# Ends of two attention stages and the expert gates behind them: an earlier start of the gate, banks of its own, last sums on GpSimd

## The reference

```
x = x + cross_attention(layernorm(x), context, mask)      # 16 heads of 16, masked
x = x + ffn(layernorm(x))     # self attention, then a hard choice of one of 8 experts
x = x + cross_attention(layernorm(x), context)            # no mask
x = x + ffn(layernorm(x))     # a hard choice by 256 gate columns, expert = column % 8

# layer 0's ffn, with h = layernorm(x, ln1)
u = h_in + attention(h) @ wo + bo                 # h_in is the ffn's input
hn2 = layernorm(u, ln2)
idx = argmax(hn2 @ gate_w + gate_b)               # 8 columns
out = u + relu(hn2 @ w1[idx] + b1[idx]) @ w2[idx] + b2[idx]

# layer 1's ffn, with h = layernorm(x)
probs = softmax(h @ Wg + bg); idx = argmax(probs)  # 256 columns
out = relu(h @ We[idx % 8] + be[idx % 8]) * probs[idx]
```

## Time and profile before

| | |
|---|---|
| median of 3 runs | 1204.88 us |
| lowest, highest | 1201.55, 1215.09 us |
| profiled execution | 1195.19 us |
| its span, first to last instruction | 1193.5 us |
| mean granted TensorE clock | 0.942 |
| PE busy | 1066.2 us (89%) |
| DVE busy | 758.1 us (64%) |
| ACT busy | 612.6 us (51%) |
| POOL busy | 222.2 us (19%) |

### The profile page before, as it was taken

How to read it: one execution, slowest core, us unless ns; L and a number is a source line. 1 busy time by engine, 2 the same in 40 slices (tenths; PEclk the granted TensorE clock), 3 DMA queues, 4 the chain that set the end, 5 groups by cost and what they waited for, 6 DMA issues and landing times. The chain is left out here.

```text
span 1193.5 us, 17937 instructions
## 1 busy us (share of the span) xinstructions
PE 1066.2 (89%) x5834; PEld 540.2 (45%) x5834; DVE 758.1 (64%) x1850; ACT 612.6 (51%) x1305; POOL 222.2 (19%) x360
## 2 busy tenths in 40 slices
PE   7989999999898999999859999996989999998380
PEld 4533333333454334444636666664633444436260
DVE  4777777876578898886542222124688988856632
ACT  2236666666432777777412333321337877783250
POOL 2000000000210314324222222202001112021255
PEclk9979999999998999999969999998979999999695
DMA  8954433330079454532750401003964333302064
GB/s 291 324 148 113 122 77 74 87 72 2 1 243 286 92 132 108 134 108 64 269 189 26 169 27 34 25 17 134 301 225 105 91 75 82 69 15 71 25 175 145
DMA packets 72922, 141.74 MB, mean 119 GB/s; under 512 B 9148, under 2 KB 26176, under 8 KB 71424
## 3 DMA queue, kind: packets, MB, share of 16 engines
q1 hardware_dynamic: 68752, 130.36, 37.1%
q0 software_dynamic: 4080, 10.23, 3.1%
HBM read 86.30 MB, written 52.17 MB: 116 GB/s over the span
## 5 line engine op out<-in xcount | busy, mean ns | idle before, releaser
L960 ACT ACTIVATE r<-ps 128x512 f32<-128x512 f32 x768 | 417.9, 599 | 185.0 <-PE ps L1074 184.2
L411 DVE TENSOR_REDUCE m<-ps 128x1 f32<-128x512 f32 x512 | 320.8, 683 | 47.0 <-PE ps L1043 47.0
L1074 PE MATMUL ps<-stacks 50*128 50x512 f32 x768 | 284.9, 461 | 7.9 <-DMA stacks<-mT 4.6
L1043 PE MATMUL ps<-stacks 48*128 48x512 f32 x720 | 286.4, 475 | 3.7 <-DVE r L488 3.0
L1083 PE MATMUL ps<-r 128*32 128x512 f32 x1536 | 208.0, 614 | 1.5 <-ACT r L960 1.5
L1074 PEld LDWEIGHTS ps<-stacks 50*128 50x128 f32 x768 | 121.1, 189 | 181.9 <-ACT r L960 126.6
L407 DVE CUSTOM_DVE_ANT_0 r<-ps,r 128x512 bf16<-128x512 f32 x256 | 165.9, 688 | 52.2 <-PE ps L1043 51.6
L1043 PEld LDWEIGHTS ps<-stacks 48*128 48x128 f32 x720 | 116.7, 192 | 24.1 <-DVE m L411 14.3
L886 POOL CAST mparts<-m 128x16 fp32r<-128x16 f32 x48 | 9.9, 206 | 550.1 <-DVE m L411 316.5
L614 ACT ACTIVATE r<-ps,cols 128x512 fp32r<-128x512 f32 x48 | 33.0, 688 | 115.6 <-PE ps L675 100.8
L675 PE MATMUL ps<-r,w 128*128 128x512 f32 x192 | 90.5, 609 | 0.5 <-issue 0.5
(11 more groups left out here) (152 smaller groups left out, 1115.8 us busy)
## 6 DMA issues: line engine op xcount, KB each, us to landing
stacks<-q_parts SPq DMA_DIRECT2D x96, 192.0 KB, 3.6
stacks<-k_parts SPq DMA_DIRECT2D x96, 192.0 KB, 4.4
k_parts<-r SPq DMA_DIRECT2D x24, 512.0 KB, 3.4
q_parts<-r SPq DMA_DIRECT2D x24, 512.0 KB, 4.4
r<-in_w SPq DMA_DIRECT2D x16, 512.0 KB, 3.6
r<-in_w SPq DMA_DIRECT2D x8, 1024.0 KB, 14.4
k_parts<-r SPq DMA_DIRECT2D x24, 256.0 KB, 4.0
q_parts<-r SPq DMA_DIRECT2D x24, 256.0 KB, 4.1
```

Of the source, the lines that this page charges most:

```text
L411: ins = dve.tensor_reduce(out, mem.ps[:, bank, :], AX.X, ALU.max)
L960: act.activation(mem.probs[:, u // HG, u % HG, :], ps[:, ST + unit_of(b, g, u) % DEEP, :], ACT.Exp, scale=SCALE).then_inc(a.p_exp.sem, 1)
L1043: pe.matmul(ps[:, led_bank(n), :], stack_of(mem.qst[g], h, ROWS)[:, t * P:(t + 1) * P], stack_of(mem.kst[g], h, ROWS), start=True, stop=Tr ...
L1074: pe.matmul(ps[:, ST + N % DEEP, :], stack_of(mem.kst[g], h, KROWS)[:, kt * P:(kt + 1) * P], stack_of(mem.qst[g], h, KROWS), start=not a.m ...
```

## The change

- Statistics of batches 0 and 1 move to places (2, 6) and (2, 9) of the last batch, those of batch 2 to (3, 9); the rows of batches 0 and 1 to (3, 2) and (3, 7). The rows of batch 2 stay between the last `normalise` and the residual. For this the rows move to the start of their region, onto query stacks, and wait until those are read.
- GpSimd's scale steps go into the attention's own order of GpSimd.
- The last batch's sum into `total_x` goes from DVE to GpSimd, and the copy into `x` is gone in `sa0`: the gate reads batch 3 from `block_in`.
- PE transposes batch 0 ahead of the last `turn`, and batch 1 ahead of the last output projection. Behind the stage PE's order is logits 0, logits 1, turn 2, logits 2, turn 3, logits 3.
- ACT's order is copies 0 in the stage, then copies 1, copies 2, exponentials 0, copies 3, exponentials 1, 2, 3.
- Each batch has a pair of banks for transposes and then logits: (0, 1), (5, 6), (2, 7), and (0, 1) again for batch 3.

```diff
-        self.rnT = [take(self.r3, C * S, [C, S]), self.w[0][:, 2:4, :, :].rearrange("p i c d -> p i (c d)")]
         self.rn = take(self.r3, NT * D, [B, T, D])
+        row_from = at[0]
+        self.rnT = take(self.r3, C * S, [C, S])
+        self.rnT_beside = [self.w[0][:, 2:4, :, :].rearrange("p i c d -> p i (c d)"),
+                           self.w[1][:, 0:2, :, :].rearrange("p i c d -> p i (c d)")]
...
+    def last_total(k):
+
+        two = slice(2 * k, 2 * k + 2)
+        pool.wait_ge(a.op_used.sem, a.op_used.at(B - 1, k + 1))
+        pool.wait_ge(a.acc_stored.sem, a.acc_stored.at(B - 1))
+        pool.tensor_tensor(mem.total_x[:, two, :], mem.x[:, B - 1, two, :], mem.block_in[(B - 1) % 2][:, two, :],
+                           ALU.add).then_inc(a.acc_ready.sem, 1)
...
+            if scale is not None and b == B - 1 and g == 3:
+                scale(0)
+                scale(1)
             if a.rows is not None and b and g >= 2:
                 sums(b - 1, g - 2)
+    if scale is None:
+        return
+    scale(2)
+    if a.self_block:
+        last_total(0)
+    scale(3)
+    if a.self_block:
+        last_total(1)
...
     products(G, NG - 1, T - 1)
+    if beside is not None:
+        meanwhile()
     turn(G)
-    meanwhile()
+    if beside is None:
+        meanwhile()
     for c in range(1, C):
         turn_out(B - 1, c, LAST_TURN[c])
+    if beside is not None:
+        beside()
     for t in range(T):
         project_out(B - 1, t, LAST_OUT[t // 2])
...
         dve.tensor_tensor(u, got, u, ALU.add).then_inc(a.op_used.sem, 1)
-        dve.wait_ge(a.op_used.sem, a.op_used.at(b, k + 1))
-        dve.wait_ge(a.acc_stored.sem, a.acc_stored.at(b))
-        dve.tensor_tensor(mem.total_x[:, two, :], x, u, ALU.add).then_inc(a.acc_ready.sem, 1)
-        dve.wait_ge(a.acc_ready.sem, a.acc_ready.at(b, k + 1))
-        dve.tensor_copy(x, u).then_inc(a.x_done.sem, 1)
...
+TURN_BANKS = ((0, 1), (5, 6), (2, 7), (0, 1))
...
     def normalise(b):
         dve.wait_ge(m.scale.sem, m.scale.at(b, 2))
+        dve.wait_ge(a.st_ps.sem, a.st_ps.at(NG * (B - 1) + b + 1))
...
+    steps = {
+        (2, 6): lambda: statistics(0),
+        (2, 9): lambda: statistics(1),
+        (3, 2): lambda: normalise(0),
+        (3, 7): lambda: normalise(1),
+        (3, 9): lambda: statistics(2),
+    }
 
     def between():
-        for b in range(1, early):
-            normalise(b)
+        normalise(2)
 
     def rest_of_batches():
-        for b in range(early, B):
-            statistics(b)
-        body(0)
-        for b in range(early, B):
-            normalise(b)
+        statistics(B - 1)
+        choose(0)
+        normalise(B - 1)
         for b in range(1, B):
-            body(b)
+            choose(b)
...
     def turned(b):
+        if b == 1 and a.self_block:
+            act.wait_ge(a.x_done.sem, a.x_done.at(B - 1))
+        if b >= 2:
+            act.wait_ge(m.g_ps.sem, m.g_ps.at(b - 1))
...
+    def rest_of_batches():
+        turned(1)
+        turned(2)
         if m.hidden is None:
             act.sem_inc(m.exps.sem, m.exps.lead)
-        turned(0)
-
-    def rest_of_batches():
-        for b in range(B):
-            body(b)
+            exps(0)
+        turned(3)
+        if m.hidden is None:
+            for b in range(1, B):
+                exps(b)
...
     def turn(b):
-        pe.wait_ge(m.rnT_ready.sem, m.rnT_ready.at(b))
+        if b == 1:
+            pe.wait_ge(a.oT_sb.sem, a.oT_sb.at(B - 1, 1))
+            pe.wait_ge(a.ot_sb.sem, a.ot_sb.at(B * NG))
+        if b == 2:
+            pe.wait_ge(a.oT_sb.sem, a.oT_sb.at(B))
+            pe.wait_ge(a.quotient.sem, a.quotient.at(B * NG))
+        if b == 3:
+            pe.wait_ge(m.logit.sem, m.logit.at(0, 2))
         pe.wait_ge(m.rn_ready.sem, m.rn_ready.at(b, 1))
...
     def begin():
-        pe.sem_inc(m.rnT_ps.sem, m.rnT_ps.lead)
         turn(0)
 
+    def beside():
+        turn(1)
+
     def rest_of_batches():
-
-        for b in range(B):
-            body(b)
-
-    return begin, rest_of_batches
+        logits(0)
+        logits(1)
+        turn(2)
+        logits(2)
+        turn(3)
+        logits(3)
```

More of the change, by code:

```diff
@@ L1202, in attend_tensor, with attend_vector @@
     pe.wait_ge(last.sem, last.at(B))
-def attend_vector(dve, a, meanwhile, beside=None):
+def attend_vector(dve, a, steps, beside=None):
     mem = a.mem
@@ L1259, in body @@
                     residual(b - 1, k)
-                if last and (g, u) in NEXT_STAGE:
-                    meanwhile[NEXT_STAGE.index((g, u))]()
+                if last and (g, u) in steps:
+                    steps[(g, u)]()
     for v in range(LEAD - UNITS):
@@ L1291, in __init__ @@
     def __init__(self, nc, stage, mem, dram, name, affine, gate_width, row, hidden, b2, weights,
-                 x_done, acc_stored, gathered, earlier, scattered=None, fetched=None, out_stored=None):
+                 before, rnT, gathered, earlier, scattered=None, fetched=None, out_stored=None):
         self.mem, self.dram, self.name, self.affine = mem, dram, name, affine
         self.width, self.row, self.hidden, self.b2 = gate_width, row, hidden, b2
-        self.weights, self.x_done, self.acc_stored = weights, x_done, acc_stored
+        self.weights, self.before, self.acc_stored = weights, before, before.acc_stored if hidden is not None else None
+        self.rnT = [mem.rnT, rnT]
         self.used = []
@@ L1344, in __init__, with tokens_after @@
             self.out_stored = Signal(out_stored, 16)
+TURN_BANKS = ((0, 1), (5, 6), (2, 7), (0, 1))
+def tokens_after(m, b):
+    a = m.before
+    return m.mem.block_in[b % 2] if a.self_block and b == B - 1 else m.mem.x[:, b, :, :]
 def gate_vector(dve, m):
@@ L1388, in body, with scale @@
         dve.tensor_copy(mem.expert[:, b, :], mem.expert_u[:, :]).then_inc(m.choice.sem, 1)
[L1390 to L1396, removed]
-            statistics(b)
-    def begin():
-        normalise(0)
+    steps = {
[5 more added lines that the diff above has]
+    }
     def between():
-        for b in range(1, early):
-            normalise(b)
+        normalise(2)
     def rest_of_batches():
-        for b in range(early, B):
-            statistics(b)
-        body(0)
-        for b in range(early, B):
-            normalise(b)
+        statistics(B - 1)
+        choose(0)
+        normalise(B - 1)
         for b in range(1, B):
-            body(b)
-    return start, begin, between, rest_of_batches
+            choose(b)
+    return steps, between, rest_of_batches
 def gate_gpsimd(pool, m):
     mem = m.mem
-    for b in range(B):
+    def scale(b):
         pool.wait_ge(m.aggr.sem, m.aggr.at(b, T))
@@ L1496, in begin @@
     def begin():
[L1497 removed]
         turn(0)
+    def beside():
+        turn(1)
     def rest_of_batches():
[L1502 to L1505 removed]
+        logits(0)
[4 more added lines that the diff above has]
+        logits(3)
+    return begin, beside, rest_of_batches
 COUNTS, TOKENS = 6, 7
@@ L2073, in _ @@
                 rest()
-                start, begin, between, rest = gate_vector(dve, me1)
-                attend_vector(dve, xa1, (lambda: start(xa1), lambda: (last_stack(xa1), begin())), between)
+                steps, between, rest = gate_vector(dve, me1)
+                attend_vector(dve, xa1, steps, between)
                 rest()
```

93 lines of the change are left out of this document (42 added, 51 removed).

## The result

The changed kernel takes 1208.34 us (median of 22 runs, 1205.68 to 1215.65), the kernel before 1202.83 (22 runs). The ratio is 1.0042, interval 1.0026 to 1.0059: 5.1 us slower, 3.1 to 7.1. I had forecast 3.9 us more, at 1208.8.

What follows compares the result with a forecast made beforehand. PE was taken to bound layer 0's gate, DVE and ACT layer 1's. Terms +1.8 and +2.1 us gave +3.9, added to the median 1204.88 for 1208.8 us; range 1199 to 1218.

Steps and rivals of the forecast that it cites:

- The sum: Whole kernel: +1.8 us in layer 0 and +2.1 in layer 1, +3.9 in all, giving 1208.8 us.
- The prediction's own signs: Both gates: later projection, earlier logits 0, PE and DVE gaps, exponentials behind copies; 37.6 us to gather, 37.4 to one-hot.
- Part 4, layer 1: Cross attention's gate: exponentials queue behind ACT's copies and delay DVE's choosing, +2.1 us, bounds 0.0 and +8.5.
- Part 4, layer 0: Self attention's gate: PE waits twice for its transposes' copies, logits 3 end later, +1.8 us, bounds -1.7 and +3.2.
- Part 2: Gate transposes moved in front: projections 0.5 and 0.3 us later, logits 0.45 earlier in layer 0, 0.6 in layer 1.
- Part 3: Last sums on GpSimd: batch 3's statistics about 1 us earlier, SP's stores issued up to 3.7 later, cost 0.
- rival 3: Layer 0: GpSimd's late addition delays SP, rows land after 614 and bound the gather, up to +3.7 us; chance 0.03.
- Parts 1 and 5: Early statistics and rows under the last attention groups, and own PSUM banks per batch in the gate: 0 each.
- The first: Level holds in layer 0, layer 1's logits start earlier without ACT queueing: -2.3 us, 1202.6; chance 0.22.
- The second: Layer 1: half clock level reaches past the last transposes, +6.4 us more, total 10.3, 1215.2; chance 0.13.
- The fourth: Change does less than said, early steps blocked; ends stay within 1 us of before, 1204.9; chance 0.07.
- The rule on transposes: Skill's rule that transposes do not bring PE's full rate; the prediction held layer 1's trace, level back by 1085, against it.

Runs made afterwards that it cites:

- pair of repeats: Kernel before and changed kernel, each run again unchanged for a second profile: ratios to the kernel before 1.0009 and 1.0026.
- the repeat of before: The kernel before, run once more unchanged for a second profile: ratio 1.0009 (0.9983 to 1.0035).
- e4: Changed kernel with ACT's increment for DVE early and ACT's old order, PE's new order kept: ratio to the kernel before 1.0015.
- e3: Changed kernel with ACT's increment for DVE early and gate transposes one batch ahead of the logits again: ratio to the kernel before 1.0012.
- e1: Changed kernel with only ACT's increment, which lets DVE begin choosing batch 0, back at the gate's start: ratio to the kernel before 1.0039.
- f1: e3 with both of GpSimd's last additions in layer 0 made ahead of batch 3's scale: ratio to the kernel before 0.9973.
- f3: f1 with four extra bf16 matmuls, results unused, at four places of layer 0's gate: ratio to the kernel before 0.9974.

## Why the prediction was right, point by point

**The sum** was right in sign and size: +3.9 us forecast, +5.1 measured (3.1 to 7.1). Its parts were not, and part of the hit is luck. In the pair of repeats layer 0 changes by -0.2 (forecast +1.8) and layer 1 by +4.25 (+2.1), so one term too high and one too low add up to 4.1 beside 3.9. That 1208.8 and 1208.34 nearly meet is luck as well: the forecast stood on 1204.88, a median of three runs, and the median of 22 is 1202.83.

**The prediction's own signs.** Two came: logits 0 right behind the residual, and the gaps in front of logits 2 and 3 in layer 0. The others did not. The output projection of layer 0 was not 0.5 later. From the last products to the first gather it took 39.4 and 38.9 us, not 37.6, and the repeat of before took 39.0. In layer 1 the exponentials of batch 0 did not follow the copies, the gap of about 2 us in front of batch 1's addition is absent, and the one-hot came 38.1 us behind the last products, not 37.4. By the words of the prediction absent gaps, and a level that differs over more than 3 us (it fell 10 to 11 us behind the copy, not 15.7), mean that its mechanism is wrong. For layer 1 it is.

**Part 4, layer 1**, +2.1 forecast; B rose by 3.5 on the mean of two profiles each, 2.8 on the first pair, 4.25 on the repeats. ACT's order was named as the cause, and it is (e4: 4.97 us with everything else kept). But the wait was another one. I had put the cost at exponentials 0 behind copies 2, and in the changed kernel those cost nothing. What costs is DVE's permission to begin, which stood in the same queue ahead of them: 6.41 us of idle DVE, 4.97 in B against e3. The exponentials behind copies, 2.07, show only once the increment is early (e1). The line stood in the diff. I had read it as bookkeeping, and followed only instructions that take time.

**Part 4, layer 0**, +1.8 forecast, bounds -1.7 and +3.2; +1.7 on the means, +3.6 by the first pair, -0.2 by the repeats. The two waits for copies came as forecast, 0.87 us each (0.7 to 1.3). The rest is where the level falls, 10 to 13 us behind the copy in the kernels without extra matmuls, 15.7 in the profile that I worked from. I called that fall steady ("the work before 590 hardly changes"); it is not, in the unchanged kernel either. So the forecast for layer 0 is not confirmed: the profiles give anything from -0.2 to +3.6, as the level fell in the kernel before.

**Part 2**, the head start, was sized too low: logits 0 were to start 0.45 and 0.6 earlier, and start 1.21 earlier in layer 0 (8.13 against 9.34) and 0.84 in layer 1 against the repeat, 2.27 against the first profile with its half level. The projection did not come later, as I had it, but 3.57 us behind the copy instead of 3.77: the transposes fill PE's waits for ACT and DVE, and I had added up the drawn lengths of pipelined groups.

**Part 3**, the sums on GpSimd: 0 forecast, and 0 in the changed kernel. The cover was PE's own lateness. With that gone (e3) the second addition cost 0.9 us in X through the cast that it blocked, and rival 3, the stores, set the gather (e3, f1, f3). **Parts 1 and 5** cost nothing that shows; no run here takes either out by itself.

**The rivals.** The first (level holds, nothing queues on ACT) failed: DVE waited 6.41 us for ACT's queue. The second failed: in layer 1 the last transposes and the projection ran at the full level in the changed kernel, 3.70 us for the projection. The third did not come in the changed kernel, whose gather followed the routing; it came once the routing was earlier (e3, f1, f3). The fourth failed: the time is 3.1 to 7.1 us longer, not the same within 1.

**The rule on transposes.** The prediction set it against the earlier trace rows. No run here decided it further, as the level fell at that place in no other profile.

## What to carry to other kernels

When a step is moved behind other work on its engine, follow the semaphore increments that stand in it as well: a "buffer is free" signal has no duration in the profile and can hold another engine for 6 us. Between two profiles of one kernel the length of layer 0's gate moved by 3 us with the clock's level, so take two profiles of each kernel before working out such a stretch from one, and compare those in which the level fell at the same distance from a common point. And a cost found to be zero is zero under the cover that the change itself builds; mend the larger wait and it comes back. A total that hits says little of its terms: look for the waits that the forecast named before calling it right.

## What the runs showed that I had not expected

- A VectorE cast of 128x4 took 1.20 and 1.21 us beside a GpSimd addition of two SBUF operands, 0.17 without.
- In two profiles of one and the same kernel, the one before, the granted clock left its full level 15.7 and 10.9 us behind the same point.
- With nothing changed behind the one-hot of layer 1, the rest of the kernel took 78.0 to 79.0 us in five profiles (both of the kernel before among them) and 82.9 to 84.6 in the other nine. In those nine GpSimd waits 1.1 to 2.0 us in front of its eleventh gather and again before later ones, in the five it does not. What it waits for is not settled.
